# Latent attention and the second gated-linear stage run as one stage, with the rotation on GpSimd

## Chip, cores and metric

One core of a Trainium2 chip runs the whole program. The metric is device time in microseconds (us), the median of the runs. All stages, loads and stores of the program are inside it.

## What is computed

The input x has 16 sequences of 256 rows of 128 numbers, 4096 rows in all. Six residual stages follow each other. The change touches the last two:

```python
x = x + 0.5 * moe0(ln(x))
x = x + gau0(ln(x))
x = x + 0.5 * moe0(ln(x))
x = x + 0.5 * moe1(ln(x))
x = x + latent_attention(ln(x))      # stage 5
x = x + 0.5 * moe1(ln(x))            # stage 6

# latent_attention, per sequence of 256 rows, 16 heads of width 8
ct_q = x @ Wd_q + b;  ct_kv = x @ Wd_kv + b
query = heads(ct_q @ Wu_q + b) + heads(rope(ct_q @ Wq_r + b, cos, sin))
key   = heads(ct_kv @ Wu_k + b) + heads(rope(x @ Wk_r + b, cos, sin))
value = heads(ct_kv @ Wu_v + b)
out   = softmax(query @ key.T / scale) @ value;   out @ Wo + b

# moe1, per row: 8 experts of width 176, 2 chosen, and one shared expert of width 352
scores = softmax(x @ gate_w.T);  w = scores * in_top2
out  = sum_e w[e] * ((silu(x @ Wg_e) * (x @ Wu_e)) @ Wd_e)
out += sigmoid(x @ shared_gate) * ((silu(x @ Wg_s) * (x @ Wu_s)) @ Wd_s)
```

## The kernel before, in words

The program writes out by hand the order of instructions of each engine, with counting semaphores between them. Stages follow each other behind a barrier (`PHASES`, `begin`, `end`). x stays in SBUF (`X`, 32 tiles of 128 rows) from the first load to the store of all 2048 KB at the very end.

**Stage 5, `at_*`, lines 1599 to 2075.** It works in 16 *elements*, one per sequence (two tiles of 128 rows). The engines run one loop over the elements, unrolled by two. In element b, TensorE (`at_pe_element`) goes through 18 head slots h = 0 to 17. At even h it computes the scores of two heads into banks 3 and 4 (L1707, `at_scores_pe`). ScalarE turns each into exponentials (L1883, one 128x512 instruction per head, into a ring `at_e` of 4). Two slots later TensorE multiplies them by the values into bank 7 (L1720, `at_values_pe`, two heads at a time, the two 128-row halves t of a head one behind the other). Between these stand steps of three neighbouring elements:

- of b-1: turning the result back (L1732), the division by the sum (L2002, L2006 on VectorE), turning again (L1739), the output matrix (L1747), adding to X (L2019);
- of b+1: splitting query and key into parts (L1962, L1966, and L1841 on ScalarE), turning keys at h = 3 and queries at h = 5 (L1644), and the *search* for each row's largest score: 16 matmul pairs from h = 7 on (L1693) into banks 1, 2, 5, each reduced by VectorE (L1975); the maxima are turned into extra rows (L1668);
- of b+2: normalising and turning x (L136, L145), the latents (L1617, L1625) and the projections (L1635), to which VectorE adds biases (L1940) before it rotates query and key (`at_project_dve`, L1946 to L1953).

**Stage 6, `sw_*`, lines 942 to 1260**, the same code as stage 4. It works in 8 *groups* of 512 rows (4 tiles). The 1760 hidden rows form 14 *chunks* of 128, chunks 0 to 10 of the routed experts and 11 to 13 shared. For each chunk TensorE computes gate rows and up rows, three 128x512 matmuls each (L988 to L990, halves of f32 split in two), into two banks each in turn. It also spreads the routing weights over the 128 rows by a matmul (L999). ScalarE applies SiLU (L1077); VectorE multiplies by the weights (L1135) and by the up rows (L1138). The down matrix follows two chunks later (L1021, 4 matmuls in two passes), accumulated in banks 4 and 5; VectorE adds the results to X (L1145, L1154). The next group's normalisation, router (L172 to L174, L188 to L217) and gates (L1006) stand between the chunks.

```python
def at_values_pe(pe, p, b, par, a):                       # L1713
    ...
    for t in range(NB2):
        ins = pe.matmul(o, p.at_v[:, par, t, a, :], p.at_e[:, a % 4, t * S:(t + 1) * S],
                        start=(t == 0), stop=(t == NB2 - 1))
```

## Time and profile before

| | |
|---|---|
| median of 3 runs | 2037.8 us (2035.96 to 2043.95) |
| profiled execution: device time | 2051.3 us |
| profiled execution: span | 2049.5 us |
| mean granted TensorE clock | 0.877 of full speed |
| TensorE matmul busy | 1669.4 us (81% of the span) |
| VectorE busy | 1242.2 us (61%) |
| ScalarE busy | 690.6 us (34%) |
| GpSimd busy | 585.8 us (29%) |

The span is that of one profiled execution, so all durations below belong to 2049.5 us, not to the median. A busy time is the union of an engine's instructions. Idle time of an engine that is not the bottleneck costs nothing. A matmul's end is modelled: its record goes on after the next one has started, so the step from start to start tells what it occupies.

### The profile page before, as it was taken

The page shows a single profiled execution, that of the slowest core. Times are in us where ns is not written, and L with a number is a line of the kernel's source. Part 1 is how long each engine was busy: PE and PEld are TensorE (multiplying, and loading weights), DVE is VectorE, ACT ScalarE, POOL GpSimd, SP SyncE. Part 2 cuts the span into 40 slices and gives each one's busy share as a digit, 9 for nine tenths or more (in the row PEclk, how much of TensorE's full clock was granted, in tenths as well). Part 3 has the DMA queues.
Part 4 walks back from the last instruction along what each step waited for, and adds up shares of the span by engine and source line. Part 5 has one row for each costly group of instructions (what it writes and reads, how often), then busy time and mean ns, then how long its engine had stood idle before and what let it go on. Part 6 is the DMA issues. An engine that isn't in the chain of part 4 may idle for free.

```text
span 2049.5 us, 36939 instructions
## 1 busy us (share of the span) xinstructions
PE 1669.4 (81%) x10156; PEld 1279.4 (62%) x10157; DVE 1242.2 (61%) x3919; ACT 690.6 (34%) x1295; POOL 585.8 (29%) x947
## 2 busy tenths in 40 slices
PE   3767994899944299929999986888888887999997
PEld 2547993455533299818888874444444444888886
DVE  2555886455544478837667655666565663666664
ACT  0114551222210055502232223544444553333331
POOL 2652665556337446741311200000000000000000
PEclk9658996899955599959999997989898997999999
DMA  5111212000001112120000000000000000000001
GB/s 206 36 41 52 60 54 89 23 19 20 10 13 41 55 50 61 45 71 12 21 10 10 11 1 1 1 1 0 0 0 0 0 0 1 1 1 0 0 1 42
DMA packets 61927, 54.32 MB, mean 27 GB/s; under 512 B 8595, under 2 KB 55060, under 8 KB 61461
## 3 DMA queue, kind: packets, MB, share of 16 engines
q1 hardware_dynamic: 52214, 34.46, 5.4%
q0 software_dynamic: 8192, 16.79, 2.8%
q10 hardware_dynamic: 1440, 2.10, 0.3%
q8 instruction: 37, 0.61, 0.1%
q14 instruction: 44, 0.36, 0.1%
HBM read 31.82 MB, written 21.50 MB: 26 GB/s over the span
## 4 chain that ended last, share of the span: by engine, by line
PE 64%; DVE 11%; issue 10%; POOL 6%; ACT 2%; DMA 2%; SPq 1%; POOLq 1%; DVEq 1%; another core or an unknown queue 0%; ACTq 0%
PE bk L1021 10%; PE bk L582 6%; PE bk L990 5%; PE bk L988 5%; PE bk L1720 5%; PE bk L989 5%; PE bk L575 3%; PE bk L1693 3%; PE bk L1707 2%; PE bk L999 2%; DVE sb_sc L1975 2%; PE bk L564 2%; PE bk L1644 2%; PE bk L566 2%; PE bk L565 2%
## 5 line engine op out<-in xcount | busy, mean ns | idle before, releaser
L112 POOL TENSOR_TENSOR sb_ln_ve<-sb_ln_mv,sb_eps 128x2 f32<-128x2 f32 (+1 forms) x48 | 9.5, 197 | 944.2 <-DVE sb_ln_mv L104 944.2
L1077 ACT ACTIVATE sb_sb_<-bk 128x512 f32<-128x512 f32 x224 | 133.4, 598 | 377.5 <-PE bk L990 372.0
L1021 PEld LDWEIGHTS bk<-sb_wd,sb_sc 128*128 128x128 f32 (+1 forms) x1792 | 233.8, 191 | 19.4
L1975 DVE TENSOR_REDUCE sb_sc<-bk 128x2 f32<-128x512 f32 x256 | 162.2, 686 | 133.7 <-PE bk L1693 133.5
L1021 PE MATMUL bk<-sb_wd,sb_sc 128*128 128x128 f32 (+1 forms) x1792 | 235.2, 274 | 0.0
L1135 DVE TENSOR_TENSOR sb_sb_<-sb_sb_,bk 128x512 f32<-128x512 f32 x176 | 120.8, 686 | 150.5 <-PE bk L999 115.8
L1883 ACT ACTIVATE sb_sa<-bk 128x512 f32<-128x512 f32 x256 | 149.0, 598 | 136.5 <-PE bk L1707 135.1
L1138 DVE TENSOR_TENSOR sb_sc<-sb_sb_,bk 128x512 f32<-128x512 f32 x224 | 153.2, 686 | 37.3 <-PE bk L990 30.6
L1720 PE MATMUL bk<-sb_sa,sb_sb_ 128*32 128x256 f32 x1024 | 153.7, 424 | 0.0
L368 POOL DMA_INDIRECT xs<-sb_xn,sb_send_row x128 | 128.8, 1006 | 87.1 <-DVE sb_send_row L357 50.8
L582 PE MATMUL bk<-sb_w2c,sb_sb_ 128*128 x1152 | 152.2, 275 | 0.0
L582 PEld LDWEIGHTS bk<-sb_w2c,sb_sb_ 128*128 128x128 f32 x1152 | 140.0, 192 | 0.2
L632 ACT ACTIVATE sb_sb_<-bk 128x512 f32<-128x512 f32 x144 | 86.0, 597 | 121.3 <-PE bk L566 121.2
L669 DVE BATCH_NORM_STATS2 sb_st<-sb_sb_ 128x6 f32<-128x512 f32 x144 | 92.8, 682 | 46.1 <-ACT sb_sb_ L632 43.9
L988 PE MATMUL bk<-sb_xh,sb_wgh 128*128 128x512 f32 x224 | 108.4, 484 | 0.0
L990 PE MATMUL bk<-sb_xl,sb_wgh 128*128 128x512 f32 x224 | 90.0, 402 | 0.5 <-issue 0.5
L990 PE MATMUL bk<-sb_xl,sb_wuh 128*128 128x512 f32 x224 | 89.8, 401 | 0.0
L989 PE MATMUL bk<-sb_xh,sb_wgl 128*128 128x512 f32 x224 | 89.6, 400 | 0.0
L989 PE MATMUL bk<-sb_xh,sb_wul 128*128 128x512 f32 x224 | 89.3, 399 | 0.2 <-issue 0.2
L988 PE MATMUL bk<-sb_xh,sb_wuh 128*128 128x512 f32 x224 | 89.5, 399 | 0.0
L638 ACT ACTIVATE sb_sb_<-bk 128x512 f32<-128x512 f32 x144 | 85.8, 596 | 10.4 <-PE bk L575 10.3
L575 PE MATMUL bk<-sb_tables,sb_sb_ 128*128 128x128 f32 x576 | 87.4, 274 | 0.1
(295 smaller groups left out, 3518.9 us busy)
## 6 DMA issues: line engine op xcount, KB each, us to landing
sb_sc<-xs SPq DMA_DIRECT2D x144, 64.0 KB, 1.8
ys<-sb_sc SPq DMA_DIRECT2D x36, 256.0 KB, 2.3
xs<-sb_xn,sb_send_row POOLq DMA_INDIRECT x128
out<-sb_X SPq DMA_DIRECT2D x1, 2048.0 KB, 8.7
sb_sa<-w SPq DMA_DIRECT2D x1, 1792.0 KB, 12.2
sb_sc<-w SPq DMA_DIRECT2D x1, 1792.0 KB, 16.9
sb_sa<-w_gu SPq DMA_DIRECT2D x1, 1760.0 KB
xs<-sb_zeros SPq DMA_DIRECT2D x24, 64.0 KB, 17.8
```

The lines of the kernel that those rows point to most:

```text
L368: pool.indirect_dma_start(p.xs, bass.IndirectOffsetOnAxis(ap=p.send_row[:, par, k, j:j + 1], axis=0), xn[:, par, j, :], None).then_inc(p.s ...
L575: ins = pe.transpose(p.bk[2 + j % 2][:, c * P:(c + 1) * P], p.r[:, j, c * P:(c + 1) * P], p.ident)
L582: ins = pe.matmul(p.bk[4 + par][:, j * P:(j + 1) * P], p.rT[:, j % 2, c * P:(c + 1) * P], p.w2c[:, bass.ds((e * FC + c) * D, D)], start=(c ...
L988: pe.matmul(bank[0:m, :], w_h[:, rows], p.xh[:, par, :], start=True, stop=False)
L989: pe.matmul(bank[0:m, :], w_l[:, rows], p.xh[:, par, :], start=False, stop=False)
L990: pe.matmul(bank[0:m, :], w_h[:, rows], p.xl[:, par, :], start=False, stop=True).then_inc(done.sem, 1)
L1021: ins = pe.matmul(bank[:, j * P:(j + 1) * P], p.hT[0:m, c % HRING, j * P:(j + 1) * P], p.wd[0:m, c * D:(c + 1) * D], start=(c in (0, NRC) ...
L1077: act.activation(p.sg[0:m, c % 2, :], p.bk[c % 2][0:m, :], ACT.Silu).then_inc(p.silu_d.sem, 1)
L1138: dve.tensor_tensor(p.hT[0:m, c % HRING, :], sg, p.bk[2 + c % 2][0:m, :], ALU.mult).then_inc(p.hid_d.sem, 1)
L1720: ins = pe.matmul(o, p.at_v[:, par, t, a, :], p.at_e[:, a % 4, t * S:(t + 1) * S], start=(t == 0), stop=(t == NB2 - 1))
L1883: act.activation(p.at_e[:, h % 4, :], p.bk[3 + h % 2][:], ACT.Exp, scale=ATT_SCALE).then_inc(p.at_ex.sem, 1)
L1975: dve.tensor_reduce(p.at_m[:, t, :].rearrange("p (q r) -> p q r", r=HQ)[:, q:q + 2, pair % HQ], p.bk[SEARCH_BANKS[f % 3]][:].rearrange("p ...
```

## The change

Stage 6 is no stage of its own any more. Its 8 groups are worked inside the elements of stage 5, group g beginning in element 2g+2. An even element carries a *front* (normalise, turn, split, shared chunks 0 and 1 of group g) and the *tail* of the group before (its last five routed chunks and its routed down matmuls). An odd element carries the *middle* (shared chunk 2, router, gates, shared down matmuls, routed chunks 0 to 5). What is left after element 15 is the tail of group 6 and all of group 7, in a row. Chunks run in the order shared, then routed (`STEP`).

Parts of it:

- **Banks.** Eight banks hold both stages: 0 for everything that is turned or small, 1 and 2 for projections, keys and searches (three search banks become two), 3 and 4 for scores, 5 for gate rows and 6 for up rows and down results (two banks each become one), 7 for values.
- **Hidden rows.** SiLU on ScalarE becomes tanh of half the gate rows; VectorE computes (tanh + 1) * gate, then times up (`fs_product_dve`, 28 operations per group where there were 25); a factor 2 goes into the gates.
- **Routing weights.** The matmul L999 is gone. The gates go to DRAM and come back by 18 broadcast transfers on SP's queue (`fs_weights_sp`); GpSimd multiplies each of the 11 routed chunks by them (`fs_weight_pool`).
- **Rotation.** The five operations after the biases go from VectorE to GpSimd (`at_rope_pool`).
- **Attention.** Values are computed four heads at a time, with t outside and the head inside; the exponentials' ring grows from 4 to 8; keys, queries and searches start at h = 6, 8 and 9.
- **Store.** Each group is stored when it is done, 256 KB at a time.

```diff
-PHASES = ["moe", "gau", "moe", "swiglu", "mla", "swiglu"]
+PHASES = ["moe", "gau", "moe", "swiglu", "mla"]
-SEARCH_BANKS = (1, 2, 5)
+SEARCH_BANKS = (1, 2)
+ERING = 8
+GBANK, UBANK = 5, 6
+TAIL_UP = {0: NSH + 6, 1: NSH + 7, 2: NSH + 8, 4: NSH + 9, 5: NSH + 10}
+TAIL_DOWN = {9: 0, 10: 1, 11: 2, 12: 3}
+FRONT_UP = {14: 0, 16: 1}
+MID_UP = {0: 2, 8: NSH, 9: NSH + 1, 11: NSH + 2, 12: NSH + 3, 14: NSH + 4, 16: NSH + 5}
+def fs_up_pe(pe, p, g, k):
...
+    pe.wait_ge(p.mul_d.sem, p.mul_d.at(n))
+    gate, up = p.bk[GBANK][0:m, :], p.bk[UBANK][0:m, :]
+    pe.matmul(gate, p.wgh[:, rows], p.fx_h, start=True, stop=False)
...
+    pe.wait_ge(p.hid_d.sem, p.hid_d.at(n))
...
+    pe.matmul(up, p.wuh[:, rows], p.fx_h, start=True, stop=False)
...
+def fs_tanh_act(act, p, g, k):
...
+    if NSH + 2 > k >= 2:
+        act.wait_ge(p.hid_d.sem, p.hid_d.at(n - 1))
+    elif k >= NSH + 2:
+        act.wait_ge(p.spread.sem, p.spread.at(NRC * g + k - NSH - 1))
...
+    act.activation(p.fsg[0:m, k % 2, :], p.bk[GBANK][0:m, :], ACT.Tanh, scale=0.5).then_inc(p.silu_d.sem, 1)
+def fs_weight_pool(pool, p, g, k):
...
+    pool.wait_ge(p.fs_wl.sem, p.fs_wl.at(16 * len(BROAD) * (g + 1)))
+    pool.wait_ge(p.hid_d.sem, p.hid_d.at(NCH * g + k + 1))
+    pool.tensor_tensor(p.fhT[c], p.fsg[:, k % 2, :], p.fhT[c], ALU.mult).then_inc(p.spread.sem, 1)
+def fs_weights_sp(sp, p, g):
...
+    sp.dma_start(p.wdr, p.fgT).then_inc(p.fs_ws.sem, 16)
+    sp.wait_ge(p.fs_ws.sem, p.fs_ws.at(16 * (g + 1)))
+    sp.wait_ge(p.r_d.sem, p.r_d.at(g))
+    for c, e in BROAD:
...
+        sp.dma_start(p.fhT[c][a:z, :], p.wdr[e:e + 1, :].to_broadcast([z - a, W])).then_inc(p.fs_wl.sem, 16)
-def at_values_pe(pe, p, b, par, a):
+def at_values_pe(pe, p, b, par, quad):
...
     for t in range(NB2):
-        ins = pe.matmul(o, p.at_v[:, par, t, a, :], p.at_e[:, a % 4, t * S:(t + 1) * S],
-                        start=(t == 0), stop=(t == NB2 - 1))
+        for r in range(HQ):
+            a = HQ * quad + r
+            o = p.bk[7][HR * r:HR * (r + 1), quad % 2 * S:(quad % 2 + 1) * S]
+            ins = pe.matmul(o, p.at_v[:, par, t, a, :], p.at_e[a % ERING][:, t * S:(t + 1) * S],
+                            start=(t == 0), stop=(t == NB2 - 1))
-    if f >= 3:
-        pe.wait_ge(p.at_mx.sem, p.at_mx.at(NH * b + f - 2))
+    if f >= 2:
+        pe.wait_ge(p.at_mx.sem, p.at_mx.at(NH * b + f - 1))
-    dve.tensor_tensor(t1, r, p.at_cos.unsqueeze(1).to_broadcast([P, 2, S]), ALU.mult).then_inc(p.at_q.sem, 1)
+    pool.tensor_tensor(t1, r, p.at_cos.unsqueeze(1).to_broadcast([P, 2, S]), ALU.mult).then_inc(p.at_rope.sem, 1)
...
+def at_pool_pair(pool, p, i, stats=(True, True), tail=None, front=None, mid=None):
...
-            out = io["out"].rearrange("(t p) d -> p t d", p=P)
-            sp.dma_start(out, p.X[:]).then_inc(p.stored.sem, 16)
+            sp.wait_ge(p.stored.sem, p.stored.at(16 * NG))
```

Three places of the new order, each with what stood there. First TensorE, the values of an element (L1720 before, L1939 now), up to what follows them. Before, in the odd element, around h = 6:

```order
L1707 MATMUL bk<-sb_w1h,sb_xl 128x256 [waits at_ex]
L1707 MATMUL bk<-sb_w1h,sb_xl 128x256 x3
L1720 MATMUL bk<-sb_sa,sb_sb_ 32x256 [waits at_ex]
L1720 MATMUL bk<-sb_sa,sb_sb_ 32x256
L1720 MATMUL bk<-sb_sa,sb_sb_ 32x256 [waits at_ex]
L1720 MATMUL bk<-sb_sa,sb_sb_ 32x256
L1739 MATMUL bk<-sb_tables,sb_sc 128x128 [waits at_on]
```

Now, TensorE in the even element, h = 4, with the turning of x (L145) and a chunk of the tail (L1658 to L1668: gate rows, then up rows) behind them:

```order
L1939 MATMUL bk<-sb_sa,sb_sb_ 32x256 x7
L1828 REGISTER_ALU [waits at_on]
L143 REGISTER_ALU [waits at_kr]
L145 MATMUL bk<-sb_tables,sb_xn 128x128 [waits ln_free]
L145 MATMUL bk<-sb_tables,sb_xn 128x128
L1656 REGISTER_ALU
L1658 MATMUL bk<-sb_w1h,sb_wgh 128x512 [waits mul_d]
L1659 MATMUL bk<-sb_w1h,sb_wgl 128x512
L1660 MATMUL bk<-sb_w1h,sb_wgh 128x512
L1661 REGISTER_ALU
L1666 MATMUL bk<-sb_w1h,sb_wuh 128x512 [waits hid_d]
```

Eight value matmuls of four heads stand together where four of two heads did, and x is turned behind a wait for VectorE's second division (`at_on`).

Second, TensorE in the odd element, h = 5 to 7: turning the result back (L1956), scores (L1924), keys (L1862), the gates (L1646), the output matrix (L1964). Now:

```order
L1956 MATMUL bk<-sb_tables,sb_sc 128x128 [waits at_on,at_xc]
L1956 MATMUL bk<-sb_tables,sb_sc 128x128
L1924 MATMUL bk<-sb_w1h,sb_xl 128x256 [waits at_ex]
L1924 MATMUL bk<-sb_w1h,sb_xl 128x256 x3
L1867 REGISTER_ALU
L1868 ISA [waits at_q]
L1862 MATMUL bk<-sb_tables,sb_sa 128x128 [waits at_hc]
L1862 MATMUL bk<-sb_tables,sb_sa 128x128 x7
L1644 ISA [waits at_ot]
L1646 MATMUL bk<-sb_tables,sb_gate 8x128 [waits rt2]
...
L2008 REGISTER_ALU
L1964 MATMUL bk<-sb_w2c,sb_sc 128x128 [waits at_ot,wt_d]
```

Before, TensorE had four value matmuls and four search matmuls between the turn (L1739) and the output matrix (L1747), and the keys stood earlier:

```order
L1739 MATMUL bk<-sb_tables,sb_sc 128x128
L1693 MATMUL bk<-sb_xh,sb_w1h 128x256 [waits at_qt]
L1693 MATMUL bk<-sb_xh,sb_w1h 128x256 x3
L1616 REGISTER_ALU
L1617 MATMUL bk<-sb_sb_,sb_w2c 128x256 [waits at_xc]
L1707 MATMUL bk<-sb_w1h,sb_xl 128x256 [waits at_ex,at_q2]
L1707 MATMUL bk<-sb_w1h,sb_xl 128x256 x3
L1720 MATMUL bk<-sb_sa,sb_sb_ 32x256 [waits at_ex]
L1720 MATMUL bk<-sb_sa,sb_sb_ 32x256
L1720 MATMUL bk<-sb_sa,sb_sb_ 32x256 [waits at_ex]
L1720 MATMUL bk<-sb_sa,sb_sb_ 32x256
L1747 MATMUL bk<-sb_w2c,sb_sc 128x128 [waits at_ot]
```

In the new order five waits on ScalarE or VectorE follow one another with one pair of heads and eight turns between them.

Third, VectorE in the odd element: between the divisions for the two halves (L2327, L2329) now stands the top-two search of the router (L188 to L204), and behind the second the gates (from L211 on), the bias, the next group's statistics, and the parts of the next query and key (L2288):

```order
L2329 TENSOR_TENSOR sb_sc<-bk,sb_sc 128x128 [waits at_on]
L185 REGISTER_ALU
L186 ISA [waits lg]
L188 COPY sb_rt_l<-bk 128x40 [waits rt2]
...
L204 TENSOR_TENSOR sb_rt_s<-sb_rt_s 128x32 [waits rt2]
L2325 REGISTER_ALU
L2327 RECIPROCAL sb_sc<-bk 128x16 [waits at_otp]
L2328 REGISTER_ALU
L2329 TENSOR_TENSOR sb_sc<-bk,sb_sc 128x128 [waits at_on]
L210 REGISTER_ALU [waits rte,gwt]
L211 TENSOR_TENSOR sb_rt_s<-sb_rt_e,sb_rt_s 128x32 [waits rt2]
...
L2288 CAST sb_sa<-sb_sb_ 128x64x8 [waits at_q2p,at_rope]
```

Before, VectorE made the parts (L1962, L1966) first of all in an element, straight after the rotation.

## Rows read from the trace of the kernel before

**Rows 1.** The page: TensorE and granted clock in 40 slices, as tenths.

```profile
PE   3767994899944299929999986888888887999997
...
PEclk9658996899955599959999997989898997999999
```

**Rows 2.** Busy time by stage: start of stage 5, its elements, stage 6's start, its groups.

```profile
core 0: us, PE busy (x) PEld busy (x) DVE busy (x) ACT busy (x) POOL busy (x), PEclk, DMA share, GB/s
...
1262.30:1730.80 468.50, 393.91 (x2832) 229.41 (x2832) 282.73 (x656) 231.60 (x469) 11.63 (x26) 0.91 0.00 0
1730.80:1746.20 15.40, 7.69 (x26) 5.82 (x26) 6.25 (x38) 3.40 (x6) 1.21 (x2) 0.50 0.00 1
1746.20:2040.40 294.20, 292.90 (x1790) 258.04 (x1790) 190.76 (x506) 94.27 (x153) 8.46 (x14) 0.99 0.00 1
```

**Rows 3.** The same columns: 14 elements together, two single elements, one group.

```profile
1262.31:1678.73 416.42, 349.60 (x2540) 204.71 (x2540) 261.75 (x607) 206.52 (x421) 11.63 (x26) 0.92 0.00 0
1291.29:1319.47 28.18, 23.28 (x184) 13.96 (x184) 18.80 (x45) 14.64 (x30) 0.90 (x2) 1.00 0.00 1
1347.82:1380.66 32.84, 28.43 (x184) 16.03 (x184) 18.89 (x44) 14.64 (x30) 0.90 (x2) 0.79 0.01 1
1818.97:1855.71 36.74, 36.74 (x230) 32.44 (x228) 24.59 (x69) 12.36 (x20) 1.21 (x2) 1.00 0.00 0
```

**Rows 4.** Timeline of TensorE in an element: start us, us, instructions.

```profile
1298.42 1.06 PE L1720 MATMUL bk<-sb_sa,sb_sb_ 128*32 128x256 f32 x8
1299.41 0.44 PE L145 MATMUL bk<-sb_tables,sb_xn 128*128 128x128 f32 x2
1299.69 1.11 PE L1644 MATMUL bk<-sb_tables,sb_sa 128*128 128x128 f32 x8
...
1423.64 0.51 PE L1693 MATMUL bk<-sb_xh,sb_w1h 24*128 24x256 f32 x6
```

**Rows 5.** The chain of waits inside a group: start us, us, step.

```profile
1867.36 0.23 PE bk L999
1867.60 0.89 PE bk L1021 x8
```

**Rows 6.** Timeline of the program's last chunk but one: gate rows, SiLU, product.

```profile
2032.58 0.48 PE L988 MATMUL bk<-sb_xh,sb_wgh 128*128 128x512 f32 x1
...
2033.55 0.60 ACT L1077 ACTIVATE sb_sb_<-bk 128x512 f32<-128x512 f32 x1 [1.68 <-PE bk L990]
...
2034.31 0.69 DVE L1138 TENSOR_TENSOR sb_sc<-sb_sb_,bk 128x512 f32<-128x512 f32 x1 [1.59 <-PE bk L990]
```

**Rows 7.** Groups of GpSimd instructions: busy us, mean ns of one.

```profile
L764 POOL TENSOR_TENSOR sb_sc<-sb_sc,sb_be2b 128x128 f32<-128x128 f32 x136 | 58.1, 460 | 8.3 <-POOL sb_sc L764 8.3
...
L1516 POOL TENSOR_TENSOR sb_X<-sb_X,sb_ga_b 128x256 f32 x10 | 7.2, 717 | 0.0
```

**Rows 8.** Timelines of VectorE (first and last step of the rotation; of the router) and of SP's queue.

```profile
1410.38 0.69 DVE L1946 TENSOR_TENSOR sb_sb_<-sb_sb_,sb_w2c 128x512 f32<-128x512 f32 x1
...
1412.51 0.69 DVE L1953 TENSOR_TENSOR sb_sb_<-sb_sb_ 128x512 f32<-128x512 f32 x1
...
1740.59 0.20 DVE L188 COPY sb_rt_l<-bk 128x40 f32<-128x40 f32 x1 [2.82 <-PE bk L174]
...
1742.45 0.19 DVE L204 TENSOR_TENSOR sb_rt_s<-sb_rt_s 128x32 f32<-128x32 f32 x1
...
28.51 0.43 SPq L2220 DMA_DIRECT2D sb_ga_bias<-ga_bias  x1
```

**Rows 9.** The page's DMA issues: KB each, median us from issue to landing.

```profile
sb_sc<-xs SPq DMA_DIRECT2D x144, 64.0 KB, 1.8
ys<-sb_sc SPq DMA_DIRECT2D x36, 256.0 KB, 2.3
out<-sb_X SPq DMA_DIRECT2D x1, 2048.0 KB, 8.7
...
sb_c2b<-b SPq DMA_DIRECT2D x1, 512.0 KB, 18.7
```

More of the change, by code:

```diff
@@ L1663, in at_maxima_rows_pe @@
     pe.wait_ge(p.at_nm.sem, p.at_nm.at(4 * b + 2 * half + 2))
-    bank = p.bk[HALF_BANKS[half]]
     for q in range(NHQ // 2):
@@ L2051, in at_dve @@
     at_project_dve(dve, p, 1, 1)
[L2052 to L2061 removed]
+    at_dve_even(dve, p, 0, 0, behind=False)
```

597 lines of the change are left out of this document (473 added, 124 removed).

## The prediction

> **What bounds the kernel now.** I read the slices of the page first [rows 1]: TensorE is busy in seven to nine tenths where the two stages lie (the last 16 slices), and the granted clock stands at .8 to .9 there. The windows by stage [rows 2] then separate two regimes. Attention is 468.5 us with TensorE busy 393.9, so 75 us of it is waiting; the groups of stage 6 are 294.2 us with 292.9 busy, so nothing there hides anything but TensorE's own work. Between them lie 15.4 us at clock 0.50 in which TensorE works 7.7. The windows by element [rows 3] give the units of my sum: fourteen elements 416.42 us, 29.74 each, and one at full clock 28.18 with TensorE busy 23.28, VectorE 18.8, ScalarE 14.6. The element at clock 0.79 takes 32.84. A group takes 36.74 us, all of it TensorE, beside VectorE 24.6 and ScalarE 12.4. So a pair of elements and one group, which the new kernel puts into one stretch, costs 2 x 29.74 + 36.74 = 96.2 us today, of which 10 us is waiting (2 x 4.9) and 3 us is clock. From the first full element (1262.3) to the end of the span (2049.5) is 787.2 us. I re-price that stretch, everything ahead of it being unchanged.
>
> **TensorE's work per pair.** The spreading of the weights goes: 11 per group at 0.23 [rows 5], 2.5 us. A group is then 34.2. The tanh, the halved factor and the other bank numbers change no matmul. The values are the second item. Today eight blocks of two heads take 0.99 from start to next [rows 4], 7.9 us per element. One such block is four instructions of 256 columns in 8 records. Eight turns of 128 columns take 1.11 in 8 records [rows 4], 0.14 each, so records of twice the columns would be 0.2 or more each, one behind the other at least 1.7 for eight (my estimate). They take 0.99. I read it as the two heads, which write different strips of 32 rows, running side by side. With t outside and four heads inside, four strips can run: 16 records in about 1.02, four blocks per element, 4.1 us, a gain of 3.8 per element. The Trainium skill ("TensorE: Matmul & The Clock Gate", Part 3) states that matmuls start and end in strict program order and that three column strips were measured 2.38 times as fast as in a row; read strictly, two heads whose passes stand one behind the other in program order gain nothing from each other today. The 0.99 for eight records speaks against that reading; it returns as a rival. An element's own work is 23.3 - 3.8 = 19.5, and a pair is 2 x 19.5 + 34.2 = 73.2 us.
>
> **VectorE, ScalarE, GpSimd.** VectorE loses the rotation, 2.8 us from the first step to the end of the last [rows 8], so a pair is 2 x 16 + 24.6 plus three products of 0.69 [rows 6], some 58 of 94 us. ScalarE is 2 x 14.6 + 12.4 = 42. Neither bounds. GpSimd gets the rotation and eleven weightings per group. It costs 460 ns at 128 columns and 717 at 256 [rows 7], 257 per 128 more, which gives 1.23 for 512. The rotation has three steps of 512 and two of 256, 5.1 us against 2.8; the weightings are 11 x 1.23 = 13.5. Per pair that is 24 us. It bounds nothing by its sum, but it is one queue: a weighting that stands behind a rotation waits up to 5 us. I cost the queue at 1.5 us per pair (in the waits below); its bounds are nothing and 5. The extrapolation's ends are 0.9 (twice 460) and 1.4 (twice 717).
>
> **The banks.** A chunk now holds one gate bank and one up bank. From the gate rows' start to the tanh is 0.97, the tanh 0.60, hand-over 0.16, product 0.69 [rows 6]: 2.42 us until the next chunk may begin. Where attention stands between two chunks this is covered; where chunks stand in a row it is the pace, against 36.74 / 14 = 2.62 for a whole chunk today. Chunks in a row thus cost no more than 2.42, with little filling.
>
> **Waits in the even element (8.3 us).** Along the new order of TensorE, with the durations above, every hand-over through VectorE or ScalarE (an instruction of 0.6 to 0.7 and its two ends) being 1.0 to 1.5: the copy of the maxima 0.7, the gate bank 0.4, x behind the second division and a chunk whose tanh waits for GpSimd 1.5, the latents' copy 0.6, the keys 1.4, the output matrix 1.3, the searches with two banks 2.4.
>
> **Waits in the odd element (11.4 us).** The maxima 0.7, the first division 1.1, the router's operations ahead of the second division 0.8 (they are 2.05 us of VectorE [rows 8]), the keys 1.5, the gates' turn 1.3, the copy of the gates 0.8, the searches' start 1.2, and the searches themselves 4.0. The searches stand at h = 9 and later in a row: a triple took 0.51, but VectorE needs a reduction per search, and with two banks in place of three every search waits for the reduction of the one before the last. Behind each waiting instruction stand the scores of the next heads, so ScalarE's exponentials move too; the ring of eight covers that, at no cost.
>
> A pair at full clock: 73.2 + 8.3 + 11.4 = 92.9. For the clock I add 1.5, half of what the pair loses today (2 x (29.74 - 28.18) = 3.1), since full-clock work of the group is mixed in. **94.4 us**, against 96.2. The ends: 88, where half of the new waits are filled by a neighbour, and 99, where each hand-over takes its upper price.
>
> **Start and end.** The slower rotation delays the start by 2.2. The first four elements hold less of the groups: 28, 28, 33 (a front only) and 45 (a first middle), 134 us. Five pairs (elements 4 to 13) are 472. Element 14 has no projection any more and is 44, element 15 has neither keys nor searches and is 37. Then the tail of group 6 and the routed part of group 7: five chunks 12.3, turn 1.0, last weighting 1.3, down matmuls 11 x 0.89 = 9.8 [rows 5]; turn and split of group 7 2.0, logits 1.3, three shared chunks and the router 9.0, shared down 2.7, eleven routed chunks 27 (2.42 each), waiting for weights 3.0, last weighting 1.3, down matmuls 9.8, last addition and store 3.0, of which a 256 KB transfer is 2.3 against 8.7 for the 2048 KB of today [rows 9]. That is 84. The 15.4 us at half clock between the stages go entirely.
>
> **Sum.** 2.2 + 134 + 472 + 44 + 37 + 84 = 773.2 against 787.2: 14.0 us less. The profiled execution took 2051.3, so it would be 2037.3. The median of the runs is 13.5 under the profiled one, so 2023.8.
>
> **The weights' trip.** Today no gates go to DRAM in this stage. SP needs 0.43 us to issue one [rows 8], 18 of them 7.7, plus a write (2.3 for 256 KB) and the last landing 1.8 (64 KB) [rows 9]: about 12 us. The first weighting is wanted about 12 us after the gates' copy, when ScalarE comes to the tanh of the third routed chunk after it. I take it as just in time, cost nothing except in the tail (3.0 above). Below nothing it cannot be. The upper end is a transfer like the 512 KB one, 18.7 us [rows 9], 7 us late. Its cover is the shared down matmuls and the first three chunks.
>
> **The rivals.**
> *Four values no faster than two (slower; chance 0.12).* If TensorE holds only two streams, a block of four costs 2 x 0.99 instead of 1.02, and the 3.8 us per element are not gained: 16 x 3.8 is 61, of which the new waits absorb some, about +50: 2075. It decides from 1.24 us per block on, where 64 blocks x 0.22 have used up the 14 us. For it: no row shows four at once. Against it: three searches, six records, in 0.51 [rows 4]. The strict reading of the skill's rule above would be this case.
> *The weights come late (0.10).* From a trip of 12 us on, every microsecond more stops the tanh, which holds the gate bank, the next chunk and the heads behind it on TensorE. At 18 us, +6 for seven groups is +42: 2066.
> *The hand-overs add up (0.16).* Five waits in a row in the odd element, each 1.0 over my price, or GpSimd's queue at its upper end: +5 to 6 per pair, +40 with the tail: 2065. For it: a queue in order passes each delay to everything behind it, and TensorE's clock fell to 0.79 in elements with gaps [rows 3].
> *Better filled (0.20).* Pairs of 88 us, the clock at full level as in the groups, 1.00 [rows 3], and the tail as priced: 6.4 less for each of the five pairs and for the two at the ends, -44: 1980. For it: 73 us of work in 94 leave room, VectorE at 58 has slack, and much of what waits stands beside independent chunks.
> *My own case (0.42)*: 10 us of TensorE's work less per pair and 15 between the stages, mostly eaten by new waits.
>
> **How the numbers follow.** 0.5% is 10 us, about what a measurement of this kernel can tell from no change. My case lies at 2024 with its own spread of some 15 us either way; of its 0.42 I give 0.25 to faster, 0.13 to same, 0.04 to slower. The better filled case is faster (0.20). The three others are 0.38, of which 0.05 ends within the bound, because the delays can be small. Faster 0.45, same 0.18, slower 0.37. The range goes from 1970, a little under the well filled case, to 2085, a little over the values' case; the likeliest case alone is 2009 to 2039. Its upper part holds three cases which would show up to 2075.
>
> **What would show it.** The distance of two even elements should be near 94 us. A block of eight value matmuls should take about 1.0 from its start to the next instruction; 2 or more is the first rival. On ScalarE a tanh of a routed chunk should not be held by the weights' transfers except in the tail. In the odd element there should be idle time of TensorE before the keys, the gates' turn, the output matrix and the searches, 1 to 1.5 each, and VectorE and TensorE in turn in the searches. TensorE's idle time should be 20 us per pair in all, its granted clock over 0.9, and the work after the last element 84 us, ending with a store of 2 to 3. I am wrong if the pair is under 90 or over 98, or if the tail is over 95.

## The result, and the profile after

| | before | after |
|---|---|---|
| median, beside each other | 2040.8 us (4 runs) | 2148.6 us (2137.3 to 2152.7, 4 runs) |
| ratio, 95% interval | | 1.0522 [1.0474, 1.0569] |
| profiled execution: device time, span | 2051.3, 2049.5 | 2152.7, 2150.6 |
| mean granted TensorE clock | 0.877 | 0.84 |
| TensorE busy | 1669.4 us | 1702.2 us |

The change makes the kernel 5.2% slower, about 108 us. I had forecast 14 us less, and a range that ended at 2085.

The page after the change: TensorE and granted clock in 40 slices, as in [rows 1].

```profile
PE   3759994899643999299999688878888888888776
...
PEclk9659996989755999599999855789898988998888
```

From slice 24 on, TensorE looks as busy as in attention before. What is new is the stretch 5, 5, 7, 8 of the clock, and that the slices of 9 and 10 tenths at the end, which belonged to stage 6, are gone.

Busy time of the changed kernel by stretch (columns as in [rows 2]): the first four elements, element 1 alone, the five pairs of elements 4 to 13, elements 5 and 6, element 12, and what follows the last exponential.

```profile
1258.57:1427.31 168.74, 137.99 (x812) 87.65 (x811) 85.24 (x204) 66.46 (x133) 31.50 (x35) 0.67 0.07 18
1294.28:1334.66 40.38, 33.44 (x183) 20.55 (x184) 18.42 (x40) 15.24 (x31) 6.38 (x7) 0.54 0.00 1
1427.31:1956.79 529.48, 439.58 (x2901) 308.53 (x2902) 317.84 (x732) 195.85 (x391) 137.73 (x133) 0.88 0.11 30
1479.08:1533.04 53.96, 42.48 (x265) 29.11 (x266) 31.18 (x81) 19.60 (x40) 12.75 (x12) 0.84 0.21 55
1533.04:1584.84 51.80, 44.84 (x317) 32.26 (x318) 32.54 (x68) 19.63 (x38) 15.08 (x15) 0.93 0.02 5
1852.40:1901.64 49.24, 41.93 (x317) 30.50 (x318) 32.67 (x68) 19.41 (x38) 15.00 (x15) 1.00 0.02 5
2045.97:2150.60 104.63, 74.73 (x376) 57.35 (x374) 39.30 (x90) 15.40 (x29) 25.09 (x21) 0.85 0.12 33
```

Three things are to be seen. A pair takes 529.48 / 5 = 105.9 us where two elements and a group took 96.2. TensorE stands idle 89.9 us of the five pairs, 18.0 per pair. And element 1, which carries no group at all, takes 40.4 us at clock 0.54, against 28.2 at 1.00 [rows 3]. The loss begins before the first group does.

What TensorE waited for in the five pairs: us in total, times, longest.

```profile
PE bk L1658 <- DVE sb_c2b L1769: 17.4, 9, 3.4
PE bk L1862 <- ACT sb_sa L2125: 12.9, 10, 1.3
PE bk L1636 <- DVE sb_sc L2329: 12.1, 5, 2.5
PE bk L1910 <- DVE sb_sc L2301: 10.9, 16, 0.8
PE bk L145 <- DVE sb_sc L2329: 5.6, 5, 1.1
```

These are the gate bank, the keys, the router's logits behind a division, the searches and x behind the second division. Windows of 3 us around the two longest waits in element 5 show what follows such a wait (TensorE's busy time is the second number, the clock the third from the end):

```profile
1479.00:1482.00 3.00, 2.52 (x16) 1.69 (x14) 2.30 (x6) 2.17 (x4) 1.60 (x2) 1.00 0.00 0
1482.00:1485.00 3.00, 0.58 (x6) 0.30 (x4) 2.95 (x5) 1.08 (x2) 2.84 (x4) 1.00 0.00 0
1485.00:1488.00 3.00, 2.57 (x18) 2.15 (x18) 1.14 (x13) 0.00 (x0) 0.75 (x1) 0.79 0.00 0
1488.00:1491.00 3.00, 3.00 (x23) 1.50 (x23) 1.13 (x8) 1.09 (x2) 0.00 (x0) 0.50 0.02 5
...
1515.00:1518.00 3.00, 0.47 (x8) 0.27 (x4) 0.15 (x1) 0.78 (x2) 2.07 (x2) 0.91 0.01 5
1518.00:1521.00 3.00, 2.41 (x6) 1.82 (x6) 2.82 (x7) 1.39 (x3) 1.69 (x2) 0.50 0.00 0
1521.00:1524.00 3.00, 3.00 (x16) 2.00 (x16) 2.56 (x4) 0.60 (x1) 1.27 (x1) 0.50 0.00 0
```

TensorE waits 2.5 us for the division (from 1482.5), and from about 1486.7 on its clock is at 0.50 (1.2 instead of 2.4 GHz), so the value block that follows takes 1.86. It waits 3.1 us for the gate bank (from 1515.5 to 1518.6), and the clock is at 0.50 from about 1517.5 to 1527.7. Behind both waits the engine is wholly busy, at half speed. The second wait leads to the routing weights: the gate rows wait until VectorE's product has read the bank, the product for ScalarE's tanh, and the tanh for GpSimd's weighting of an earlier chunk. The chain of waits of that stretch (start us, us, step):

```profile
1463.51 1.00 PE bk L1939 x16
...
1488.77 1.86 PE bk L1939 x16
...
1499.95 0.59 ACT sb_sc L1704
1500.57 1.44 DMA wdr<-sb_sc
1502.02 0.34 SPq L1810
...
1511.03 0.43 SPq L1810
1511.49 4.27 DMA sb_w2c<-wdr
1515.95 0.11 POOL sb_w1l_f L1799
```

From the gates' copy in ScalarE (ending 1500.5) to the first weighting on GpSimd (1515.95) it is 15.4 us: 1.4 to write, 9.4 to issue 18 transfers (0.52 each), 4.3 until the last has landed.

### The profile page after: what moved, and what is told of

Same layout as the page of the kernel before. It is cut to its first block, busy times and chain, and to the rows that moved or that the text cites. A ratio compares the mean times of both kernels' runs of the same rounds, so it can differ in the third digit from the quotient of the medians.

```text
span 2150.6 us, 36749 instructions
## 1 busy us (share of the span) xinstructions
PE 1702.2 (79%) x10068; PEld 1293.9 (60%) x10069; DVE 1247.7 (58%) x3847; ACT 672.4 (31%) x1280; POOL 782.7 (36%) x1115
## 4 chain that ended last, share of the span: by engine, by line
PE 54%; issue 14%; DVE 10%; POOL 10%; ACT 4%; DMA 3%; SPq 2%; POOLq 1%; DVEq 1%; another core or an unknown queue 0%; ACTq 0%
PE bk L1675 6%; PE bk L582 6%; PE bk L1021 5%; PE bk L575 3%; PE bk L990 3%; PE bk L1939 3%; PE bk L988 2%; PE bk L989 2%; PE bk L1910 2%; POOL sb_w1l_f L1799 2%; PE bk L1924 2%; POOL xs L368 2%; DVE sb_sc L2301 2%; PE bk L1862 2%; PE bk L564 2%
## 5 line engine op out<-in xcount | busy, mean ns | idle before, releaser
L1799 POOL TENSOR_TENSOR sb_w1l_f<-sb_c2b,sb_w1l_f 128x512 f32<-128x512 f32 x64 | 81.0, 1275 | 313.1 <-DMA sb_w2c<-wdr 233.0
L1769 DVE SCALAR_TENSOR_TENSOR sb_c2b<-sb_c2b,bk 128x512 f32<-128x512 f32 (+1 forms) x112 | 76.7, 685 | 136.4 <-ACT sb_c2b L1717 135.9
L1717 ACT ACTIVATE sb_c2b<-bk 128x512 f32<-128x512 f32 (+1 forms) x112 | 66.9, 597 | 215.0 <-PE bk L1660 151.5
L1077 ACT ACTIVATE sb_sb_<-bk 128x512 f32<-128x512 f32 x112 | 66.3, 598 | 191.4 <-PE bk L990 188.7
L632 ACT ACTIVATE sb_sb_<-bk 128x512 f32<-128x512 f32 x144 | 86.0, 597 | 121.2 <-PE bk L566 121.1
L1021 PEld LDWEIGHTS bk<-sb_wd,sb_sc 128*128 128x128 f32 (+1 forms) x896 | 116.9, 191 | 9.6
L1021 PE MATMUL bk<-sb_wd,sb_sc 128*128 128x128 f32 (+1 forms) x896 | 117.6, 274 | 0.0
L2167 ACT ACTIVATE sb_sa<-bk 128x512 f32<-128x512 f32 x128 | 71.4, 596 | 96.7 <-PE bk L1924 96.6
L1658 PE MATMUL bk<-sb_w1h,sb_wgh 128*128 128x512 f32 (+1 forms) x112 | 60.8, 543 | 46.8 <-DVE sb_c2b L1769 46.6
L638 ACT ACTIVATE sb_sb_<-bk 128x512 f32<-128x512 f32 x144 | 85.9, 597 | 10.7 <-PE bk L575 10.6
L1138 DVE TENSOR_TENSOR sb_sc<-sb_sb_,bk 128x512 f32<-128x512 f32 x112 | 76.3, 686 | 15.3 <-PE bk L990 12.3
L575 PEld LDWEIGHTS bk<-sb_tables,sb_sb_ 128*128 128x128 f32 x576 | 70.3, 141 | 18.1 <-issue 4.7
L1675 PE MATMUL bk<-sb_wd,sb_w1l_f 128*128 128x128 f32 x512 | 70.3, 294 | 5.6 <-POOL sb_w2c L1799 5.6
```

What stands on the lines that cost most here:

```text
L575: ins = pe.transpose(p.bk[2 + j % 2][:, c * P:(c + 1) * P], p.r[:, j, c * P:(c + 1) * P], p.ident)
L632: act.activation(p.r[:, j, :], p.bk[j % 2][:], ACT.Relu).then_inc(p.act_r.sem, 1)
L638: act.activation(p.rT[:, j % 2, :], p.bk[2 + j % 2][:], ACT.Copy).then_inc(p.act_t.sem, 1)
L1021: ins = pe.matmul(bank[:, j * P:(j + 1) * P], p.hT[0:m, c % HRING, j * P:(j + 1) * P], p.wd[0:m, c * D:(c + 1) * D], start=(c in (0, NRC) ...
L1138: dve.tensor_tensor(p.hT[0:m, c % HRING, :], sg, p.bk[2 + c % 2][0:m, :], ALU.mult).then_inc(p.hid_d.sem, 1)
L1675: ins = pe.matmul(p.bk[UBANK][:, j * P:(j + 1) * P], p.fhT[c][0:m, j * P:(j + 1) * P], p.wd[0:m, c * D:(c + 1) * D], start=(c == chunks[0] ...
```

## The experiments

Each kernel ran beside runs of the kernel before on the same chip; the kernel before had medians from 2023.6 to 2053.8 on different chips, so the ratios are compared, not the microseconds. The changed kernel itself stands at 1.0522 [1.0474, 1.0569], and the difference of two ratios carries the noise of both, some 0.6% or 12 us. "Clock" is that of whole elements in the attention (for fused kernels, of the five pairs); before it is 0.92 [rows 3].

| run | ratio to before [95%] | us per element or pair | clock |
|---|---|---|---|
| e1 head by head | 1.0521 [1.0485, 1.0556] | pair 106.0 | 0.88 |
| e2 four heads alone | 1.0347 [1.0310, 1.0384] | element 34.6 | 0.64 |
| e3 no broadcasts | 1.0271 [1.0238, 1.0305] | pair 101.7 | 0.90 |
| e4 fillers | 1.0383 [1.0350, 1.0417] | pair 101.5 | 0.93 |
| e5 four heads twice | 1.0530 [1.0494, 1.0565] | element 36.8 | 0.79 |
| e6 fillers before the keys | 1.0040 [1.0015, 1.0066] | element 30.6 | 0.89 |
| e7 four heads and fillers | 1.0111 [1.0076, 1.0146] | element 30.7 | 0.79 |
| e8 changed kernel, two heads | 1.0521 [1.0485, 1.0556] | pair 107.0 | 0.93 |
| e9 attention only | (no stage 6) | element 40.9 | 0.54 |
| e10 rotation and late turns alone | 1.0424 [1.0386, 1.0463] | element 35.7 | 0.71 |
| e11 weights in three parts | 1.0312 [1.0267, 1.0356] | pair 101.9 | 0.91 |
| e12 late fillers | 1.0112 [1.0075, 1.0149] | element 31.2 | 0.93 |
| e13 old turns, fused | 1.0751 [1.0696, 1.0806] | pair 115.2 | 0.78 |
| e14 old turns, weights in three parts | 1.0650 [1.0602, 1.0698] | pair 116.0 | 0.76 |
| e15 e14 with two heads | 1.0860 [1.0821, 1.0899] | pair 118.0 | 0.83 |
| e16 late turns alone | 1.0371 [1.0339, 1.0402] | element 35.1 | 0.72 |
| e17 three parts and fillers | 1.0211 [1.0190, 1.0233] | pair 98.7 | 0.96 |
| e18 rotation on VectorE, fused | 1.0526 [1.0504, 1.0548] | pair 105.4 | 0.88 |

### Four heads a block

e2 puts only this part of the change into the kernel before; e1 swaps the two loops in the changed kernel's block (head outside, half inside).

```diff
     for t in range(NB2):
-        ins = pe.matmul(o, p.at_v[:, par, t, a, :], p.at_e[:, a % 4, t * S:(t + 1) * S],
+        for r in range(HQ):
+            h = HQ * a + r
+            ins = pe.matmul(p.bk[7][HR * r:HR * (r + 1), a % 2 * S:(a % 2 + 1) * S], p.at_v[:, par, t, h, :],
+                            p.at_e[h % 8][:, t * S:(t + 1) * S], start=(t == 0), stop=(t == NB2 - 1))
```

> The kernel before with nothing changed but the values: four heads a block, half outside, head inside, ring of eight. Work theory: 3.8 us less of TensorE's work per element; an element has 4.9 us of waiting already, so two thirds of the saving arrive, 35 to 60 us faster than before. Clock theory: an element with 19.5 us of work in 28 keeps the full clock less often than one with 23.3; elements at 0.5 to 0.8 appear, and the time is between 20 us faster and 60 us slower than before, with the mean clock in the attention stage well under 0.91.

1.0347: some 70 us slower, just above the clock theory's 60, by an edit that takes 3.8 us of work out of every element. Elements 1 to 13 of e2, then a value block at half clock (timeline; 1.0 at full):

```profile
1286.49:1735.85 449.36, 373.08 (x2367) 230.65 (x2368) 245.35 (x570) 193.19 (x390) 10.69 (x24) 0.64 0.00 0
```

```profile
1710.82 1.94 PE L1721 MATMUL bk<-sb_sa,sb_sb_ 128*32 128x256 f32 x16
```

The work theory falls. TensorE waits 5.9 us per element instead of 4.8 (the mean of [rows 3]), and at a mean of 0.64 it spends seven tenths of the element at half clock. Where it waits in one element, before and in e2 (the keys, the first search):

```profile
PE bk L1644 <- DVE sb_sa L1966: 1.7, 1, 1.7
PE bk L1693 <- ACT sb_w1h L1846: 0.3, 1, 0.3
...
PE bk L1644 <- DVE sb_sa L1966: 2.6, 1, 2.6
PE bk L1693 <- ACT sb_w1h L1846: 1.3, 1, 1.3
```

Both waits are longer by 0.9 to 1.0 us, one block of two heads. Before, values were computed at h = 2 and h = 6, ahead of the keys (h = 3) and of the first search (h = 7); four at a time they come at h = 4 and h = 8, behind them. So the edit does more than remove work: it takes the work away that stood in front of two waits.

> The changed kernel with the value matmuls in the old order (head outside, half inside), still four heads behind one wait. Clock theory: the new kernel's excess over the forecast is the granted clock, which falls after stretches in which TensorE idles; giving TensorE more to do per block (a block near 2.0 us at full clock instead of 1.0) is partly paid back by a higher clock, so the time changes by less than half of 64 x 1.0 = 64 us, 0 to +30 us, with the mean clock up from 0.84. Work theory: TensorE's own work sets the time, so it is +50 to +64 us at an unchanged clock. If the block stays at 1.0 us, the engine reorders nothing and runs four strips anyway, and the time is the same.

```profile
1551.12 1.09 PE L1939 MATMUL bk<-sb_sa,sb_sb_ 128*32 128x256 f32 x16
```

The last case came: the block takes 1.09 to its modelled end (1.07 in the changed kernel), whatever the order inside. A second block of e1, whose heads 4 and 5 are read from `g2b` and heads 6 and 7 from `be2b`, shows how:

```profile
1508.31 0.42 PE L1939 MATMUL bk<-sb_g2b,sb_sb_ 128*32 128x256 f32 x2
1508.34 0.42 PE L1939 MATMUL bk<-sb_be2b,sb_sb_ 128*32 128x256 f32 x2
1508.55 0.39 PE L1939 MATMUL bk<-sb_g2b,sb_sb_ 128*32 128x256 f32 x2
```

Each head has four records in all. The kernel writes all of head 4, then all of heads 5, 6 and 7. The records start otherwise: two that read `g2b`, two that read `be2b`, and so on in turn, four times over. No run puts waits between the four heads, so what a wait there would cost is not shown; two heads, each behind a wait of its own, already took 0.99 for their eight records [rows 4].

> The kernel before with four heads a block, each block computed twice over (the second pass overwrites the first), 64 more blocks of 1.0 us than e2_before_four_heads (2109.7). Clock theory: TensorE has its old work per element back (23.3 us), the granted clock of the attention stage returns from 0.64 to about 0.9, and the time falls by 50 to 75 us, to 2035 to 2060, although 64 us of work are added. Any theory in which work adds time: 2110 to 2174.

```diff
-    for t in range(NB2):
+    for t in range(2 * NB2):
+        t = t % NB2
```

A miss: 1.0530 against e2's 1.0347. The clock came back to 0.79 only, and the element went from 34.6 to 36.8. So it isn't the smaller amount of work that costs. The wait ahead of the keys is still 2.6 us, since the added work stands behind it, and the clock falls there, as three windows of 2 us show (and twice more in the same element):

```profile
1313.00:1315.00 2.00, 0.76 (x7) 0.52 (x5) 1.92 (x4) 0.36 (x1) 0.00 (x0) 1.00 0.01 4
1315.00:1317.00 2.00, 0.51 (x3) 0.52 (x4) 1.85 (x7) 1.21 (x3) 0.00 (x0) 0.77 0.00 0
1317.00:1319.00 2.00, 2.00 (x11) 1.55 (x9) 1.59 (x9) 0.00 (x0) 0.15 (x1) 0.50 0.00 0
```

e7 therefore fills the waits themselves: nine matmuls ahead of the keys, four ahead of the first search.

```diff
+                fill(pe, p, p.bk[1], 9)
                 at_keys_pe(pe, p, b + 1)
+            if h == 7:
+                fill(pe, p, p.bk[5], 4)
```

> e2_before_four_heads (2109.7) with nine matmuls that nothing needs ahead of the keys (TensorE waits 2.6 us there) and four ahead of the first search (1.3 us): 3.0 us at full clock per element. Clock theory: most elements at full clock and below the 28.2 of the kernel before, 26 to 28, so 20 to 45 us faster than the kernel before, 1995 to 2020; if the fillers don't suffice, the clock stays at 0.7 to 0.9 and the time at 2040 to 2080. Without the clock: 2110 or more.

1.0111 against e2's 1.0347: some 48 us faster by adding 3.0 us of useless work per element, ahead of the two waits that e2 had lengthened. Elements 2 to 13:

```profile
1302.77:1671.37 368.60, 327.02 (x2341) 209.70 (x2342) 226.23 (x525) 175.95 (x360) 9.80 (x22) 0.79 0.00 0
```

The mechanism is shown. Of the expected cases the second came, fillers that don't suffice: the clock still fell among the searches.

e8 computes two heads at a time again in the changed kernel:

```diff
-        if h >= HQ and h % HQ == 0:
-            at_values_pe(pe, p, b, par, h // HQ - 1)
+        if h >= LAG and h % 2 == 0:
+            at_values_pe(pe, p, b, par, h // 2 - 1)
```

> The changed kernel with the values two heads at a time, at every even h, as before the change; the ring of eight and all else stay. Clock theory: 3.8 us more of TensorE's work per element, but a fuller engine; elements 0 and 1 return from 36 and 40 us to under 32, the others gain clock about as they gain work: 15 to 50 us faster than the changed kernel, at a mean clock over 0.87. Work theory: 40 to 60 us slower.

The time is that of the changed kernel. (The profiled execution, 2148.4 us, was the longest of e8; its median is 2129.4, so the pair of 107.0 is some 0.9% high.) Its even elements are all at clock 1.00 and 51.6 us, where the one even element of the changed kernel at 1.00 takes 49.2. So four heads do save 2.3 us at equal clock, and the clock takes them back. A gain was expected and none came; elements 1 and 2 even lengthened (43 and 46 us, against 40 and 40).

### The attention's order, without and with the groups

e9 leaves the groups out of every element:

```diff
 def at_pe_element(pe, p, b, par, behind=True, ahead=2, tail=None, front=None, mid=None):
+    tail = front = mid = None
```

> The changed kernel with no groups in it: stage 6 is left out whole, the output is x after the attention; the attention's order, banks, rotation on GpSimd and four-head values are as in the changed kernel. The kernel before has 458.9 us from its first exponential to its last, 28.7 per element. If the attention's own new order is what lowers the clock, its elements are 34 to 37 us at a clock near 0.6 and the attention takes 550 us, 90 more than before: then most of the 107 us lost is not due to the groups. If the fusion is the cause, the elements are at 27 to 30 us.

It leaves out stage 6. Elements 3 to 13:

```profile
1376.19:1826.26 450.07, 372.34 (x2003) 227.61 (x2004) 202.84 (x426) 167.71 (x330) 70.00 (x75) 0.54 0.01 3
```

40.9 us per element, above the 34 to 37 expected, with no single wait over 1.4 us. Two of these and a group of 36.7 would be 118.5 (116 with a group of 34.2, without the spreading); the fused pair takes 105.9. Putting the groups between the heads is a gain of 10 to 13 per pair over the same attention by itself. So the attention's new order, by itself, loses 11 us per element; in the fused pairs the groups fill part of its waits. Of its parts, e10 and e16 put the later turns into the kernel before, e10 together with the rotation on GpSimd:

> The kernel before with the rotation on GpSimd and keys, queries and searches at h = 6, 8 and 9 instead of 3, 5 and 7; values two heads at a time, three search banks, stage 6 apart. TensorE's work is that of before. If this part of the change costs (GpSimd's 6.4 us for the rotation, searches that end three heads later), 10 to 40 us slower with the projection waiting for the last search; if it is neutral, as I forecast for it, within 10 us of before.

> The kernel before with keys, queries and searches at h = 6, 8 and 9, the rotation left on VectorE. If the later turns cause the 85 us of e10 (searches end three heads later, the projection waits for the last one, and all that follows is serial), it is 50 to 90 us slower than before. If GpSimd's rotation is the cause, 0 to 20 us slower.

```diff
-            if h == 3:
+            if h == 6:
                 at_keys_pe(pe, p, b + 1)
-            elif h == 5:
+            elif h == 8:
                 at_queries_pe(pe, p, b + 1)
-            if 7 <= h < NH - 1:
-                for f in range(2 * (h - 7), 2 * (h - 6)):
+            if 9 <= h <= NH:
+                for f in range(2 * (h - 9), 2 * (h - 8)):
```

(ScalarE's copies and VectorE's first searches move with them.) e16 alone costs 3.7% (76 us), as expected. e10, which adds the rotation on GpSimd and the parts later on ScalarE and VectorE, costs 4.2% (86 us), twice what I had thought at most. The later turns are nearly all of it: the two intervals overlap. Elements 1 to 13 of e16, and what TensorE waited for there:

```profile
1293.95:1749.62 455.67, 391.85 (x2367) 227.03 (x2368) 245.14 (x570) 194.76 (x390) 10.73 (x24) 0.72 0.00 0
```

```profile
PE bk L1693 <- DVE sb_sc L1975: 28.6, 39, 0.8
PE bk L1635 <- DVE sb_sc L1975: 17.9, 13, 1.4
```

TensorE idles 63.8 us in 13 elements, 4.9 each, as before (4.8 in the mean of [rows 3], 4.9 in the element at full clock). Only the places differ: the wait ahead of the keys is gone, and the searches' waits and 1.4 us ahead of the projection now stand together at the end of the element. The same work and the same idle time, and the clock is 0.72 instead of 0.92. So the amount of idle time does not tell the clock; its distribution matters.

e18 takes the rotation back to VectorE in the changed kernel:

```diff
-    if stats[1] or stats[0]:
-        at_rope_pool(pool, p, 2 * i + 2)
...
         dve.tensor_tensor(dst, src, bias, ALU.add).then_inc(p.at_q.sem, 1)
+    at_rope_dve(dve, p, b)
```

> The changed kernel with the five operations of the rotation on VectorE, behind the biases; keys, queries and searches stay at h = 6, 8 and 9. If the rotation on GpSimd is nearly free or a help, as I forecast, 0 to 20 us slower than the changed kernel (2.8 us more for VectorE per element); if GpSimd's queue is what delays the keys, 10 to 30 us faster.

No difference clear of noise (1.0526). The rotation on GpSimd took 1.28 per step of 512 columns, near the 1.23 priced, and where it runs is worth nothing here.

e13 adds to e18's edit the old h of keys, queries and searches on TensorE and ScalarE, and moves VectorE's parts and searches forward:

```diff
+    at_parts_dve(dve, p, b + 1)
     up(tail, NSH + 6)
...
-    at_parts_dve(dve, p, b + 1)
     up(tail, NSH + 10)
```

> The changed kernel, fused, with the rotation back on VectorE, keys, queries and searches at h = 3, 5 and 7 as before the change, the parts first in VectorE's element; two search banks, four-head values and the weights' trip stay. If the later turns are what starves TensorE (e10 lost 85 us by them alone), the elements without groups come from 36 to 41 us to 34 (as in e2) or less and the pairs from 105.7 to 98 to 101: 40 to 80 us faster than the changed kernel. If the groups had filled those waits already, the same time within 15 us.

The opposite came: 2.2% slower than the changed kernel. e14 (1.0650) and e15 (1.0860) rest on the same edit. Waits in an odd element of e13:

```profile
PE bk L1636 <- DVE sb_sc L2330: 4.2, 1, 4.2
PE bk L1646 <- ACT sb_sc L2159: 2.5, 1, 2.5
```

With the parts ahead on VectorE, the division comes later: the logits wait 4.2 us instead of 2.5, the gates' turn 2.5 instead of 1.1. In the fused kernel, with this order of VectorE, the old turns are worse than the late ones. An order that has the old turns and the early division too was not tried.

> e13_after_old_turns with the 18 transfers of the weights on three semaphores as in e11. Both undone causes are apart in place (h = 3 to 8 and h = 11 to 14 of an odd element), so they add: 25 to 40 us faster than e13, at or a little under the kernel before.

> e14 with the values two heads at a time again: 3.8 us more of TensorE's work per element. In the changed kernel this made no difference (e8), because the clock gave back what the work cost. If the same holds, within 15 us of e14; if e14 already runs at full clock, 20 to 50 us slower than e14.

The three parts gained 1% of e13 (21 us, where 25 to 40 were expected), half of what they gain below, and none of it in the pairs (116.0 against 115.2): it all lies in the last two elements and behind them. Two heads cost 2% (43 us). That is the number of e15's second case, but not its condition: e14 did not run at full clock (0.76).

### The weights' trip

e3 leaves the 18 transfers out:

```diff
-    for c, e in BROAD:
-        sp.dma_start(p.fhT[c][a:z, :], p.wdr[e:e + 1, :].to_broadcast([z - a, W])).then_inc(p.fs_wl.sem, 16)
...
-    pool.tensor_tensor(p.fhT[c], p.fsg[:, k % 2, :], p.fhT[c], ALU.mult).then_inc(p.spread.sem, 1)
+    pool.tensor_tensor(p.fhT[c], p.fsg[:, k % 2, :], p.fsg[:, k % 2, :], ALU.mult).then_inc(p.spread.sem, 1)
```

> The changed kernel without the 18 broadcast transfers per group; GpSimd multiplies the tanh-gated rows by themselves instead of by the routing weights, so this leaves out the routing weights of the routed experts. Theory of the late weights: the trip takes 15.4 us where 12 were forecast, TensorE's wait of 3.1 us on the gate bank in each odd element goes and with it the half clock behind it (about 10 us at 0.5, worth 5): 7 to 8 us per group and 5 to 15 in the tail, 60 to 75 us faster than the changed kernel. Clock theory alone, the weights being a side matter: the 3.1 us go but other waits keep the clock down, 20 to 30 us faster.

1.0271: 2.5% of the kernel before, 51 us, are the trip, between the two cases expected. In the profiled executions 21 us of it lie in the five pairs, 11 in elements 14 and 15 and 14 behind them (the part after the last exponential went from 104.6 to 90.9). e11 keeps all transfers and only splits the wait for them, which parts late weights from the transfers' own load:

```diff
-    pool.wait_ge(p.fs_wl.sem, p.fs_wl.at(16 * len(BROAD) * (g + 1)))
+    pool.wait_ge(sem.sem, sem.at(16 * sum(c in LOADED[part] for c, e in BROAD) * (g + 1)))
```

> The changed kernel with three semaphores for the 18 transfers (chunks 0 and 1; 2 to 5; 6 to 10), so that the first weighting waits for 3 of them instead of 18. Theory of the late weights: the first weighting comes about 7 us earlier, TensorE's 3.1 us wait in the odd element and the half clock behind it go, as in e3_after_no_broadcast: 35 to 55 us faster than the changed kernel. If the time of e3 came from the transfers' own load instead (memory traffic beside the work), nothing changes.

All 18 transfers are made, and the time is 1.0312, within noise of e3, so their own load costs little. The chain of waits in one odd element:

```profile
1511.51 1.44 DMA wdr<-sb_sc
...
1512.97 0.34 SPq L1813
...
1513.36 0.41 SPq L1813
...
1513.82 4.42 DMA sb_w1l_f<-wdr
...
1518.42 1.26 POOL sb_w1l_f L1802
```

6.9 us instead of 15.4, and in that element the gate bank is no longer among TensorE's waits. This wait is shown as one cause, worth about 43 us, give or take 13.

### Filling the waits

e4 puts matmuls that nothing needs ahead of the waits of the changed kernel:

```diff
+def fill(pe, p, b, n):
+    pe.wait_ge(p.at_q.sem, p.at_q.at(NS1 * (b + 1) + 4))
+    for _ in range(n):
+        pe.matmul(p.bk[1][:], p.wgh[:, 0:P], p.wgh[:, 0:W], start=True, stop=True)
```

> The changed kernel with matmuls that nothing needs (512 columns, 0.23 us each at full clock, into bank 1 while it stands free), ahead of four waits: 9 ahead of the router's logits, 4 ahead of x in an even element, 5 ahead of the keys: 14 per odd and 9 per even element, 2.1 to 3.2 us of added work per element, all where TensorE waited. Clock theory: the half-clock stretch that follows the wait for the logits and that which follows the keys go or shrink, 3 to 7 us per pair, 20 to 50 us faster than the changed kernel although it computes more. Any theory without the clock: the same time or up to 30 us slower.

1.0383, 28 us faster with more work in it. In the five pairs the wait ahead of the logits falls from 12.1 us to 0.9, those ahead of the keys are gone, and the clock goes from 0.88 to 0.93; the wait for the gate bank stays (15.3). Together with the earlier weights:

> The changed kernel with the weights in three parts (e11) and the fillers of e4 ahead of the logits, x and the keys. e11 gained 2% and e4 1.4% of the changed kernel's time; if they are separate causes the gains add, 60 to 80 us faster than the changed kernel, 1.010 to 1.025 of the kernel before, with pairs near 98 us. If both had removed the same half-clock stretch, no more than e11 alone (1.03).

```profile
1408.76:1902.21 493.45, 439.65 (x3016) 305.97 (x3017) 317.91 (x732) 195.22 (x391) 138.50 (x133) 0.96 0.13 32
```

1.0211: 63 us or 3.1% of the kernel before less than the changed kernel, nearly the sum of the two (2.1 and 1.4), as expected for separate causes. The pair is 98.7 at clock 0.96, with 5.3 us of fillers in it. It stays 2.1% slower than the kernel before, above all in the first three elements, which still take 114 us at 0.63 to 0.69. The same remedy in the kernel before, `fill(pe, p, p.bk[1], 6)` ahead of the keys in e6 and three at each of h = 12, 13 and 14 in e12:

> The kernel before and nothing else changed than six matmuls that nothing needs (512 columns into bank 1, 1.4 us at full clock) in each element, ahead of the keys, where TensorE waits 1.7 us. Clock theory: the elements of 30.3 and 32.9 us (clock 0.89 and 0.79) become ones of 28.2 at 1.00, 12 to 22 us faster than before. Without the clock: the same time, or some us slower.

> The kernel before with nine matmuls that nothing needs per element (three each at h = 12, 13 and 14, into bank 0), among the searches and the last scores, in front of the place where the clock fell in the elements of 30 to 33 us; 2.1 us at full clock where TensorE waits 1.3 us. If the clock goes by what TensorE does there, all elements reach 1.00 and 28.2 to 28.9 us, 5 to 20 us faster than before; if it doesn't, 0 to 15 us slower.

Both missed: 0.4% and 1.1% slower. In e6 the clock still fell, in the second half of elements, well behind the filled wait; in e12 the elements at 1.00 took 29.4 instead of 28.2, since the fillers delayed the searches, and the clock fell in others. In the kernel before, whose longest wait is 1.7 us, filling these waits gained nothing. No version that I ran beats the kernel before.

## Where the prediction was right and wrong

The forecast end of the span was 2035.5, the measured 2150.6, 115.1 later. By the terms of my sum:

| term | forecast | measured | difference |
|---|---|---|---|
| first full element begins | 1264.5 | 1258.6 | -5.9 |
| elements 0 to 3 | 134 | 168.7 | +34.7 |
| five pairs | 472 | 529.5 | +57.5 |
| element 14 | 44 | 52.0 | +8.0 |
| element 15 | 37 | 37.2 | +0.2 |
| the rest | 84 | 104.6 | +20.6 |

The measured rows are cut at the first exponential of an element, which in the kernel before came at 1265.3, 3 us behind my 1262.3. In equal marks the start would be 9 us early and elements 0 to 3 some 38 too long.

**Right.** The value block (1.02 forecast, 1.00 measured), with the reading that strips run side by side. By the Trainium skill ("TensorE: Matmul & The Clock Gate", Part 3), matmuls start and end in program order. The records of e1 don't agree for heads in different strips: written head by head, they start by turns between heads 4 and 5 and heads 6 and 7. Here the measurement decides. Whether the engine or the translation of the kernel changed the order no run tells.

**The sum of the waits, in part by luck.** 19.7 per pair forecast, 18.0 measured, and all at places that I had named. But the gate bank took 3.5 per pair where I had 0.4 and a share of 1.5, the logits 2.4 where I had 1.1 for the division, and the searches 3.2 where I had 7.6. The errors cancelled.

**Wrong: the clock.** The step was "For the clock I add 1.5, half of what the pair loses today (...), since full-clock work of the group is mixed in". At a mean clock of 0.88, a quarter of the five pairs' time is at half clock. If TensorE was busy all through it, that lost 0.12 x 529.5 = 64 us, 12.7 per pair. This upper bound is 11.2 more than priced, of the 11.5 that a pair took too much (the late weights below bring part of it about). TensorE's busy time says the same: 87.9 us per pair where I had 73.2 of work. In elements 0 and 1, which hold no group, I priced 28 us each; they ran at 0.54 to 0.55 and took 36 and 40, 20 of the 34.7 us. Elements 2 and 3 took 7 and 8 more than priced, at 0.63 and 0.87. [Rows 3] had shown that clock 0.79 makes an element 4.7 us longer. I used the clock as an addition to the waits, not as something that the new waits themselves set. e2, e4, e7, e16 and e17 show that they do.

**Wrong: "I take it as just in time".** The weights' trip takes 15.4 us, not 12: the last landing took 4.3, against 1.8 for the 64 KB of [rows 9], and the 18 issues 9.4 instead of 7.7; only the write was shorter (1.4 for 2.3). The rival with late weights had the mechanism, at 0.10. That its price of 42 us is near what e11 gained (43) is luck: 42 stood for a trip of 18 us, and at 15.4 its rule gives 3.4 us for each of seven groups, 24 us. The rest is what it left out, the half clock behind each of these waits. Late weights also explain a part of the tail: it is 7.5 us shorter in e11 and 14 in e3, of the 20.6 too much.

**Wrong: the value of saved work.** I counted 3.8 us per element as gain. In the kernel before, four heads a block cost 70 us (e2), in the changed kernel they are worth nothing (e8). It isn't the saving itself that costs (e5 put the work back behind the waits and got slower still), but that the values no longer stand ahead of the keys and of the first search (e7 filled these places and won 48 us back). My rival for the slower side asked whether four strips are possible, and they are; none asked which waits the saved work had covered.

**The down matmuls**: 22 records in 2.65 per tile, 10.6 per group against 9.8 priced, 0.8 of the pair.

The range was too narrow because no case in it let the clock of the whole stage fall. What stays open: why elements with the same idle time in other places are granted 0.72 or 0.92, and why the attention by itself sits at 0.54 without recovering. That filling waits raises the clock is shown; the rule behind it is not. The late turns and four-head values each cost much by themselves in the kernel before (76 and 70 us); how they share the 11 us per element that e9 shows was not taken apart. In the changed kernel, taking either back did not help (e8 the same time, e13 slower), so which part of the order sets its clock is not shown. Late weights and fillable waits together are 63 of the 107 us that the ratio stands for. Of the other 44 it is known only where they lie: by the terms of the table, e17 is still 28 us over the forecast in elements 0 to 3 and 21 in the five pairs.
